# The last stage of an eight-step transformer kernel: fewer spaced gathers, paired inverse roots, the last half's sums ahead of its product, two PSUM banks for the shared product

## The reference, cut to what matters

```python
scores = softmax(flat @ router_w.T + router_bias)            # 32 experts
topk_scores, topk_idx = top_k(scores, 4); topk_scores /= topk_scores.sum()
h = silu(flat @ gate_w[e].T) * (flat @ up_w[e].T)             # hidden size 128
expert_out = h @ down_w[e].T
out = (expert_out[topk_idx] * topk_scores).sum(over the 4 experts)
out = out + (silu(flat @ sgate_w.T) * (flat @ sup_w.T)) @ sdown_w.T   # "shared" part, hidden size 512
x = layernorm(x + out)
```

## Time and profile before

| | |
|---|---|
| median of 3 runs | 1296.8 us |
| the profiled execution's own time | 1300.21 us |
| its span, first to last instruction | 1298.4 us |
| busy: PE, DVE, ACT, POOL | 1010.7, 811.9, 547.4, 489.5 us |
| mean granted TensorE clock, share of full speed | 0.877 |
| gathers at L116 and L2727 (`f_got`) | 64 and 64 |
| first and last gather at L2727, start | 1193.22 and 1286.62 us |

### The profile page before, as it was taken

One profiled execution on the slowest core, in us unless ns is written; L12 is line 12 of the kernel. 1 busy time (PEld: TensorE's weight loads), 2 busy tenths in 40 slices (PEclk: granted clock), 3 DMA queues, 4 the chain that ended last, 5 costly groups with the idle time before them and its releaser, 6 DMA issues. The chain is left out here.

```text
span 1298.4 us, 20321 instructions
## 1 busy us (share of the span) xinstructions
PE 1010.7 (78%) x6768; PEld 602.2 (46%) x6768; DVE 811.9 (63%) x2127; ACT 547.4 (42%) x878; POOL 489.5 (38%) x484
## 2 busy tenths in 40 slices
PE   5772119952589899989989998988788989997971
PEld 3662016741234344434434443443247878874541
DVE  3757860132677788787887878688727443555643
ACT  1341004422136556665556665464464433431241
POOL 4101145525515410352004530143435544556776
PEclk8985558986569799997999999798899999999995
DMA  4225403421322211231122312353127756641122
GB/s 114 66 65 162 74 11 92 120 63 40 103 74 55 76 33 46 47 107 40 41 60 53 101 49 78 84 142 135 46 78 209 216 165 170 174 124 39 45 76 65
DMA packets 113122, 114.88 MB, mean 88 GB/s; under 512 B 17813, under 2 KB 95253, under 8 KB 109781
## 3 DMA queue, kind: packets, MB, share of 16 engines
q1 hardware_dynamic: 73830, 74.07, 20.7%
q0 software_dynamic: 12048, 25.71, 7.2%
q10 hardware_dynamic: 27144, 13.83, 3.7%
HBM read 67.94 MB, written 41.94 MB: 85 GB/s over the span
## 5 line engine op out<-in xcount | busy, mean ns | idle before, releaser
L2158 DVE TENSOR_REDUCE maxima<-psum 128x1 f32<-128x512 f32 (+4 forms) x624 | 385.5, 643 | 109.7 <-PE psum L1973 57.3
L2096 ACT ACTIVATE probs<-psum 128x1024 f32<-128x1024 f32 (+3 forms) x384 | 299.2, 809 | 271.9 <-PE psum L1992 206.4
L2006 PE MATMUL psum<-probs,v_wide 128*32 128x512 f32 (+3 forms) x1536 | 175.9, 532 | 0.0
L1969 PE MATMUL psum<-ka,qa 75*128 75x512 bf16 (+3 forms) x440 | 145.7, 344 | 28.4 <-DVE maxima L2158 22.8
L1481 POOL DMA_INDIRECT sorted<-x_rows,to_row x76 | 75.5, 993 | 209.3 <-ACT probs L2096 114.0
L2517 ACT ACTIVATE g_silu<-psum 128x512 f32<-128x512 f32 x80 | 47.8, 598 | 177.3 <-PE psum L2423 101.0
L1988 PE MATMUL psum<-qa,ka 78*128 78x512 bf16 (+3 forms) x440 | 118.4, 334 | 4.7 <-DMA qa<-max_parts 2.4
L1407 POOL DMA_INDIRECT w_gu<-expert_out,to_row x64 | 65.4, 1022 | 136.8 <-ACT probs L2096 95.3
L1969 PEld LDWEIGHTS psum<-ka,qa 75*128 75x128 bf16 x440 | 42.9, 99 | 129.5 <-DVE maxima L2158 111.0
L2423 PE MATMUL psum<-w_gu,g_xT 128*128 x384 | 95.4, 391 | 9.1 <-DVE g_h L2593 5.4
L116 POOL DMA_INDIRECT f_got<-expert_out,dense x64 | 63.9, 998 | 68.2 <-DMA f_got<-expert_out,dense 43.7
(11 more groups left out here) (333 smaller groups left out, 1825.7 us busy)
## 6 DMA issues: line engine op xcount, KB each, us to landing
g_rows<-sorted SPq DMA_DIRECT2D x192, 64.0 KB
expert_out<-g_y ACTq DMA_DIRECT2D x48, 256.0 KB
qa<-q_steps SPq DMA_DIRECT2D x30, 192.0 KB
ka<-k_steps SPq DMA_DIRECT2D x10, 576.0 KB
w<-in_W SPq DMA_DIRECT2D x16, 256.0 KB, 3.1
w_gu<-in_gu SPq DMA_DIRECT2D x4, 1024.0 KB, 10.7
sorted<-blank SPq DMA_DIRECT2D x54, 64.0 KB
q_steps<-w_gu SPq DMA_DIRECT2D x12, 256.0 KB
```

What stands on the lines that cost most here:

```text
L1969: mm = pe.matmul(bank[:, h * width:h * width + plain], qa[b][0:ROWS_MAX, h0 + h, qt * P:(qt + 1) * P], ka[b][0:ROWS_MAX, h0 + h, seg * HAL ...
L2006: mm = pe.matmul(B[OUT][32 * h:32 * (h + 1), q0 - c * HALF:HALF], v_wide[s.buf][:, j, h, PAD * (1 - c):PAD * (1 - c) + 32], probs[k % PRIN ...
L2096: act.activation(probs[k % PRING][:, 2 * pair:2 * pair + 2, 0:w], PS[:, 2 * pair:2 * pair + 2, 0:w], ACT.Exp).then_inc(exps, 1)
L2158: dve.tensor_reduce(maxima[:, seg, h0:h0 + heads, qt], bank[:, 0:heads * width].rearrange("p (h k) -> p h k", h=heads), AX.X, ALU.max).the ...
```

## The change

```diff
-PACED_HALVES = 4
+PACED_HALVES = 3
-NORMS_BESIDE = {19: 0, 21: 1, 23: 2, 25: 3, 27: 4, 29: 5}
-SCALED_BESIDE = {(6, 0): 0, (6, 2): 1, (7, 0): 2, (7, 1): 3, (7, 3): 4}
+NORMS = ((0, 2), (2, 4), (4, 6), (6, 7))
+NORMS_BESIDE = {24: 0, 28: 1}
+SCALED_BESIDE = {(6, 1): 0, (6, 2): 1, (7, 2): 2, (7, 3): 3}
...
+        SHARED_OUT = (OUT_BANK, XT_BANK)
+        LAST_OUT = (SHARED_OUT[(HALVES - 1) % 2], HT_BANK)
...
-                for first, last in ((0, HALF_TILES - 1), (HALF_TILES - 1, HALF_TILES)):
+                for first, last in ((0, HALF_TILES // 2), (HALF_TILES // 2, HALF_TILES)):
...
                 def emit_out(i):
                     pe.wait_ge(h_done, chunk_unit(i, HC1))
-                    wait_past(pe, F.acc_done, i)
+                    wait_past(pe, F.acc_done, i - 1)
                     for t in range(HALF_TILES):
+                        second = i == HALVES - 1 and t >= HALF_TILES // 2
+                        bank = LAST_OUT[1] if second else SHARED_OUT[i % 2]
...
+                        if t == HALF_TILES - 1 or i == HALVES - 1 and t == HALF_TILES // 2 - 1:
+                            mm.then_inc(F.y_psum, 1)
...
                 def emit_normed(i):
-                        act.wait_ge(shift_done, i + 1 if i < HALVES - 1 else HALVES + (j == HALF_TILES - 1))
+                        no = [first <= i < last for first, last in NORMS].index(True) if i < HALVES - 1 else (
+                            len(NORMS) + (j >= HALF_TILES // 2))
+                        act.wait_ge(shift_done, no + 1)
...
                 def emit_sums(i, q):
                     if i < PACED_HALVES:
                         wait_landed(dve, got_landed, (i * HALF_TILES + 2 * q + 2) * K1)
+                    elif i == HALVES - 1:
+                        for t in (2 * q, 2 * q + 1):
+                            dve.wait_ge(tile_landed[t], K1 * 16)
...
-                def emit_tile(i, t):
-
-                    at = i * HALF_TILES + t
-                    dve.wait_ge(tile_landed[t], K1 * 16)
...
+                def emit_last(piece):
+
+                    i, first = HALVES - 1, piece * HALF_TILES // 2
+                    part = slice(first, first + HALF_TILES // 2)
+                    rows = acc[:, i * HALF_TILES + first:i * HALF_TILES + first + HALF_TILES // 2, :]
+                    dve.wait_ge(F.y_psum, HALVES + piece)
+                    order.done(dve.tensor_tensor(rows, LAST_OUT[piece].rearrange("p (t n) -> p t n", t=HALF_TILES)[:, part, :],
+                                                 rows, ALU.add))
+                    for j in range(first, first + HALF_TILES // 2):
+                        last = dve.bn_stats(stats[:, j, :], acc[:, i * HALF_TILES + j, :])
+                    order.done(last)
+                    for j in range(first, first + HALF_TILES // 2):
+                        last = dve.bn_aggr(mv[:, j, :], stats[:, j, :])
+                    order.done(last)
+                    order.done(dve.tensor_scalar(less_mean[:, i, part], mv[:, part, 0], -1.0, None, ALU.mult))
+                    dve.tensor_scalar(var_eps[:, i, part], mv[:, part, 1], EPS, None, ALU.add).then_inc(var_done, 1)
...
                 emit_out(HALVES - 2)
-                dve.wait_ge(F.y_psum, HALVES)
-                for t in range(HALF_TILES):
-                    emit_tile(HALVES - 1, t)
+                for q in range(2):
+                    emit_sums(HALVES - 1, q)
+                for piece in range(2):
+                    emit_last(piece)
...
-                def emit_rstd(i, first, last):
+                def emit_rstd(no):
+
+                    if no < len(NORMS):
+                        halves, part = slice(*NORMS[no]), slice(0, HALF_TILES)
+                        pool.wait_ge(var_done, NORMS[no][1])
+                    else:
+                        first = (no - len(NORMS)) * HALF_TILES // 2
+                        halves, part = slice(HALVES - 1, HALVES), slice(first, first + HALF_TILES // 2)
+                        pool.wait_ge(var_done, HALVES + no - len(NORMS))
...
-                for i in range(len(NORMS_BESIDE), HALVES - 1):
-                    emit_rstd(i, 0, HALF_TILES)
-                emit_rstd(HALVES - 1, 0, HALF_TILES - 1)
-                emit_rstd(HALVES - 1, HALF_TILES - 1, HALF_TILES)
+                for no in range(len(NORMS_BESIDE), len(NORMS) + 2):
+                    emit_rstd(no)
```

More of the change, by code:

```diff
@@ L2451, in emit_out @@
                     pe.wait_ge(h_done, chunk_unit(i, HC1))
-                    wait_past(pe, F.acc_done, i)
+                    wait_past(pe, F.acc_done, i - 1)
                     for t in range(HALF_TILES):
+                        second = i == HALVES - 1 and t >= HALF_TILES // 2
+                        bank = LAST_OUT[1] if second else SHARED_OUT[i % 2]
                         for c in range(HC1):
-                            mm = pe.matmul(OUT_BANK[:, t * C:(t + 1) * C], F.hT[:, c, t * P:(t + 1) * P], F.w_d[:, c, :],
-                                           start=(t == 0 and c == 0), stop=(c == HC1 - 1), skip_group_check=True)
-                    mm.then_inc(F.y_psum, 1)
+                            mm = pe.matmul(bank[:, t * C:(t + 1) * C], F.hT[:, c, t * P:(t + 1) * P], F.w_d[:, c, :],
+                                           start=(t % (2 if second else HALF_TILES) == 0 and c == 0), stop=(c == HC1 - 1),
+                                           skip_group_check=True)
+                        if t == HALF_TILES - 1 or i == HALVES - 1 and t == HALF_TILES // 2 - 1:
+                            mm.then_inc(F.y_psum, 1)
                 def emit_chain(kind, c):
@@ L2624, in emit_out @@
                     dve.wait_ge(F.y_psum, i + 1)
-                    dve.tensor_tensor(acc[:, half_of(i), :], OUT_BANK.rearrange("p (t n) -> p t n", t=HALF_TILES),
+                    dve.tensor_tensor(acc[:, half_of(i), :], SHARED_OUT[i % 2].rearrange("p (t n) -> p t n", t=HALF_TILES),
                                       acc[:, half_of(i), :], ALU.add).then_inc(F.acc_done, 1)
@@ L2727, in gather @@
                         pool.indirect_dma_start(oob_is_err=False, **transfer).then_inc(here, 16)
-                def emit_rstd(i, first, last):
-                    part, no = slice(first, last), i + (first > 0)
-                    pool.wait_ge(var_done, i + 1 if i < HALVES - 1 else i + last)
-                    pool.tensor_tensor(rstd[:, i, part], var_eps[:, i, part], G.minus_half[:, part], ALU.pow).then_inc(rstd_done, 1)
+                def emit_rstd(no):
[6 more added lines that the diff above has]
+                        pool.wait_ge(var_done, HALVES + no - len(NORMS))
+                    out, power = rstd[:, halves, part], G.minus_half[:, 0:HALVES * HALF_TILES].rearrange(
+                        "p (i t) -> p i t", i=HALVES)[:, halves, part]
+                    pool.tensor_tensor(out, var_eps[:, halves, part], power, ALU.pow).then_inc(rstd_done, 1)
                     pool.wait_ge(rstd_done, no + 1)
-                    pool.tensor_tensor(shift[:, i, part], less_mean[:, i, part], rstd[:, i, part], ALU.mult).then_inc(shift_done, 1)
+                    pool.tensor_tensor(shift[:, halves, part], less_mean[:, halves, part], out, ALU.mult).then_inc(shift_done, 1)
                 for i in range(FINISH[LAST - 1].paced, K1 * TB):
@@ L2758, in _ @@
                         if i * HALF_TILES + t in NORMS_BESIDE:
-                            emit_rstd(NORMS_BESIDE[i * HALF_TILES + t], 0, HALF_TILES)
-                for i in range(len(NORMS_BESIDE), HALVES - 1):
-                    emit_rstd(i, 0, HALF_TILES)
-                emit_rstd(HALVES - 1, 0, HALF_TILES - 1)
-                emit_rstd(HALVES - 1, HALF_TILES - 1, HALF_TILES)
+                            emit_rstd(NORMS_BESIDE[i * HALF_TILES + t])
+                for no in range(len(NORMS_BESIDE), len(NORMS) + 2):
+                    emit_rstd(no)
 class Shared:
```

## The result

| | before | changed |
|---|---|---|
| median, 20 runs each | 1297.02 us (1289.51 to 1307.43) | 1289.18 us (1282.54 to 1300.06) |
| ratio, 95% interval | 1 | 0.9938 [0.9916, 0.9960] |
| span of the profiled execution | 1298.4 us | 1287.8 us |

The change makes the kernel faster by 8 us, with an interval of 5.2 to 10.9; the forecast was 10.4. The spans of the two traces differ by 10.6 us. Both traces happen to reach the mark from which the prediction counts, the last gather of half 2, at the same time (1162.68 and 1162.72), so what follows can be laid side by side.

What follows compares the result with a forecast made beforehand. POOL's gather issue stream, plus the work behind the last landing, was taken to bound the kernel's end. Terms -8.4 - 5.8 + 3.8 = -10.4 us, applied to the median 1296.8, gave 1286.4 us, range 1284 to 1291.

Steps and rivals of the forecast that it cites:

- Half 3: POOL's gathers of half 3 without spacing: 17 pitches at 1.30 us, so half 4 starts 8.4 us earlier.
- The hole of 2 us at 1188.60: POOL idle among half 3's spaced gathers; if POOL's own and not the spacing's, half 3 gains only 6.4 us.
- Norms in the stream: Among POOL's gathers six norms of 1.76 us go and two of 2.37 come in: net 5.8 us saved.
- The 0.7 hole at 1264.42: Extra gap of 0.7 us in POOL's gather stream; the forecast kept it but said it may go.
- Behind the last landing: After the last gather lands, DVE 3.1, POOL 0.15, ACT 0.40 and the store 0.2 us more: 3.8 us later.
- Cover: Slack of other engines: DVE 6.3 us in the worst case before its last tiles, ACT 1.6 us at the end.
- ACT's added wait: Ahead of scaling half 2 at chunk (7, 2); might hold that silu to near 1258.3, no later than before; worth nothing.
- ACT's cover at the end: ACT scales 12 rows from 1275.3 to 1280.2, last two released at 1281.8: 1.6 us of cover, nothing counted.
- DVE's bound: Worst case, nothing of the shared part moves: DVE's sums (7, 0) end at 1268.7, 6.3 us before 1275.0.
- Port: Rival: DVE and POOL block each other at the end over a shared SBUF port pair; 1288.0 us, chance 0.06.
- the first two rivals: Half 3's hole stays or two-tile passes are dear: 1288.4 or 1290.0, chance 0.18; DVE and POOL collide: 1288.0, chance 0.06.

Runs made afterwards that it cites:

- u1: Changed kernel with half 3's 16 gathers spaced again; 1295.30 us, ratio 0.9982 to the kernel before.
- u2: Changed kernel with POOL's power and product one half at a time again, six among the gathers; 1294.83 us, ratio 0.9971 to the kernel before.
- u3: Changed kernel with the eighth half handled tile by tile as before; 1285.61 us, ratio 0.9894 to the kernel before.
- u4: Changed kernel with DVE's first piece (tiles 0 and 1) ahead of the sums of tiles 2 and 3; 1288.40 us, ratio 0.9912 to the kernel before.
- again: The changed kernel itself measured a second time, nothing altered; 1289.18 us, ratio 0.9915 to the kernel before.
- u5: Changed kernel with the shared product in one bank again, PE waiting for DVE as before; 1290.14 us, ratio 0.9939 to the kernel before.
- q1: Changed kernel with all gathers unspaced and DVE's sums moved out of places where they hold PE; 1274.19 us, ratio 0.9818 to the kernel before.
- q2: q1 with the eighth half's first piece ahead of the last two tiles' sums; 1272.18 us, ratio 0.9789 to the kernel before.
- p0: Changed kernel with no gather spaced, all 128 unspaced; 1283.48 us, ratio 0.9890 to the kernel before.

## Why the prediction was right

- **Half 3, 8.4 us.** 8.35 in the trace (1193.22 to 1184.87), 8.2 in u1. The hole of 2 us at 1188.60 went with the spacing.
- **Norms in the stream, 5.8 us.** 6.8 in the trace: from half 4's first gather to the last issue 86.61 us where it was 93.40. The 0.7 hole at 1264.42 is gone, and the two norms cost 2.27 us each (pitches of 3.49 and 1.38 where two of 1.30 would stand) and not 2.37. Less than 0.1 is left over. u2 gives 5.9.
- **Behind the last landing, 3.8 us later.** DVE's sums and two passes end 5.76 us after they start (5.82 expected; a pass is 1.54, not 1.61). From last issue to E it is 3.58 us longer, where the terms without the store make 3.6. The stores of 128 KB land 1.9 us after their issue in the median, 0.3 more than that of 64 KB (0.2 expected). But from E to the end of the span it is 5.99 where it was 5.03, so 0.96 us more. This piece is 3.5 to 7.3 us over the twelve traces with no pattern that I can give, so what the store adds to it cannot be sized from one execution of each.
- **The match is in part luck.** Measured between the two traces the terms are -8.35, -6.79, +3.58 and +0.96, together -10.6. The stream gave 1.0 us more than forecast and the end took 0.7 more, and the two nearly cancel.
- **Cover.** DVE had 7.2 us left, 6.3 expected in the worst case (the terms named there end at 1268.5, not 1268.7). ACT's added wait held the last silu until 1258.08 (1258.3 expected) and cost nothing. ACT's cover at the end was 0.66 us and not 1.6: the prediction counted 12 rows, but the two of the eighth half's first piece come ahead of the last two as well. DVE's bound held the start of the shared part fixed against the gathers. It is not: u3 and u4 show that the slack can be gone. That was the prediction's real gap, and it mattered to the experiments more than to the result.
- **Port.** Here the row beat the Trainium skill's rule ("SBUF — State Buffer", "SBUF: two separate sides"). The rule has the later of two such operations wait for the whole of the first. DVE's two multiply-adds at 1274.08 take 0.61 us beside the end of a POOL power (until 1274.18) and a product, and the six behind them 1.92, beside another power of 1.10. From first to last that is 2.56 us, as at 1264.13 before, where POOL ran no power beside it. POOL pays little: the product of eight columns at that place takes 0.22 to 0.35 us in the traces where DVE's last sums start beside it (changed, again, u1, u5, q1, q2), and 0.20 where nothing runs beside it. No operation stood for the length of the other.
- **The size.** The sum said 10.4, the two traces 10.6, the two measurements 7.8 and 10.3 between medians. What pulls them apart is probably spread ahead of and behind the changed part (from the 24th silu to the 25th, 9.5 to 15.2 us; the piece after E, 3.5 to 7.3); that is argued and not shown. I could not show more than that the forecast lies in both intervals. The 2.8 us between the forecast of 1286.4 and the median of 1289.18 have no cause on record, and the range of 1284 to 1291 was drawn from a spread of three runs (0.6 below and 2.1 above), where 20 runs of the kernel before spread from 1289.5 to 1307.4. By the median alone the first two rivals (1288.0 to 1290.0) are as near as the forecast; it is the traces that rule them out, with no hole in half 3, passes of 1.54 us and no block at the port.

## What to carry to other kernels

Where one engine issues work as fast as it can up to the end, every instruction between two issues is worth its full time, and pairing small operations pays as long as their results are not wanted in between. Price what is pushed behind the last arrival just as carefully: here a quarter of the gain (3.6 of 15.1 us) went there, and a backlog on another engine (ACT's 14 rows) bounds what undoing that would bring. Then ask which path is second: with the gathers 15 us faster it was only 0 to 7 us behind, and the next gain (q1) lay in moving both. And compare traces from marks inside the changed stage, since what lies ahead of it and behind it moved by several us between executions here.

## What was not expected of the hardware

PE's clock fell or held after nearly the same idle time. In the changed kernel PE stood 3.10 us and two products then took 1.13; in its second run it stood 3.07 and they took 2.06, at the low level (1.2 GHz), and the stretch from 1180 to 1189 shows a granted clock of 0.81, where the first trace shows 1.00. Ahead of it PE was busy alike in both: without a stop from 1176 to 1180, and 4.82 of the 6 us before that. Changed kernel, then second run:

```profile
1184.73 1.13 PE L2450 MATMUL psum<-xT_all,sg_sb 128*128 128x512 f32 x2 [3.10 <-DVE s_hT L2609]
```

```profile
1183.59 2.06 PE L2450 MATMUL psum<-xT_all,sg_sb 128*128 128x512 f32 x2 [3.07 <-DVE s_hT L2609]
...
1180.00:1189.00 9.00, 5.93 (x12) 2.39 (x11) 4.62 (x13) 1.19 (x2) 6.98 (x7) 0.81 0.21 53
```

In the nine traces of the changed kernel and its variants that have sums in those places, the first two periods are of three kinds: 13.8 us at a granted clock of 1.00 (changed, 1188 to 1202), 15.3 to 15.7 at 0.89 (u1, 1187 to 1202; u5, 1176 to 1191) and 16.7 to 17.0 at 0.80 (u4, 1196 to 1213; p0, 1176 to 1193). So the low level costs the shared part 1.5 to 3.2 us a time, which is free while gathers end last and not in p0. In q1, where PE stands for 0.9 us at most in those places, both kinds of loss are gone: the granted clock from 1164 to 1262 is 0.99.
